# Attention and Fourier block on one core: first keys and queries loaded by themselves, part of it from ScalarE's queue, statistics split

## What is computed

```
xn  = layernorm(x)
q   = rope(xn @ wq)      16 heads of 16 channels
k,v = rope(xn @ wk), xn @ wv     4 heads of 16 channels, query head h uses key head h % 4
a   = softmax(causal(q k^T / 4)) @ v ;  attention = a @ wo
f   = real(ifft(fft(xn) @ (w_re + i w_im))) + bias
out = x + attention + f
```

## Time and profile before

| | us |
|---|---|
| median of three executions | 992.09 |
| the profiled execution | 994.67 |
| its span, first to last instruction | 993.0 |
| TensorE busy in the span | 946.6 |
| VectorE, ScalarE, GpSimd busy | 731.2, 653.1, 312.9 |
| mean granted clock of TensorE | 0.969 |

### The profile page before, as it was taken

One profiled execution on the slowest core, in us unless ns is written; L12 is line 12 of the kernel. 1 busy time (PEld: TensorE's weight loads), 2 busy tenths in 40 slices (PEclk: granted clock), 3 DMA queues, 4 the chain that ended last, 5 costly groups with the idle time before them and its releaser, 6 DMA issues.

```text
span 993.0 us, 17699 instructions
## 1 busy us (share of the span) xinstructions
PE 946.6 (95%) x6764; PEld 463.8 (47%) x6764; DVE 731.2 (74%) x894; ACT 653.1 (66%) x1302; POOL 312.9 (32%) x343
## 2 busy tenths in 40 slices
PE   8969999999999989999999999999999999999998
PEld 6744555445444334534454555444444443544424
DVE  6887677678777897787888666677778887788801
ACT  6423666646667746676777666676677765677795
POOL 4368863865238000136300223236111000100000
PEclk9858999999999989999999999999999997999999
DMA  7535132154101300010100321001410000000000
GB/s 249 134 75 92 34 85 77 34 102 112 50 7 54 60 17 1 13 49 22 49 19 3 69 58 33 22 1 34 104 37 1 2 2 1 13 11 2 1 1 22
DMA packets 37700, 43.48 MB, mean 44 GB/s; under 512 B 11376, under 2 KB 23280, under 8 KB 37616
## 3 DMA queue, kind: packets, MB, share of 16 engines
q1 hardware_dynamic: 37544, 42.35, 17.5%
q10 hardware_dynamic: 72, 0.01, 0.0%
HBM read 27.13 MB, written 14.68 MB: 42 GB/s over the span
## 4 chain that ended last, share of the span: by engine, by line
PE 46%; ACT 4%; issue 1%; DVE 1%; POOL 0%; ACTq 0%; POOLq 0%
PE psO L1387 17%; PE psS L1370 10%; PE psA L1323 10%; ACT prob_sb L986 3%; PE psS L1355 2%; PE psS L1357 1%; PE psA L1328 1%; PE psA L1370 1%; PE psA L1338 1%; PE psS L1296 1%; ACT oraw_sb L995 1%; PE psS L1347 0%; DVE pmax L1132 0%; PE psS L1303 0%; PE psA L1402 0%
## 5 line engine op out<-in xcount | busy, mean ns | idle before, releaser
L986 ACT ACTIVATE prob_sb<-psS 128x512 f32<-128x512 f32 (+2 forms) x1108 | 561.3, 589 | 210.6 <-PE psS L1370 207.7
L1134 DVE TENSOR_REDUCE pmax<-psA 128x2 f32<-128x1024 f32 x384 | 459.9, 1220 | 111.5 <-PE psA L1323 110.4
L1370 PE MATMUL psS<-q_st,k_st 50*128 50x512 f32 (+3 forms) x1232 | 392.1, 425 | 4.6 <-ACT prob_sb L986 3.8
L1323 PE MATMUL psA<-k_st,q_st 48*128 48x512 f32 (+3 forms) x1280 | 360.4, 426 | 16.5 <-DVE pmax L1132 5.6
L1387 PE MATMUL psO<-prob_sb,v_sb 128*17 128x512 f32 (+3 forms) x2560 | 301.7, 543 | 16.2 <-ACT prob_sb L986 7.8
L1323 PEld LDWEIGHTS psA<-k_st,q_st 48*128 48x128 f32 x1280 | 177.5, 193 | 242.0 <-DVE pmax L1134 87.6
L1132 DVE TENSOR_REDUCE pmax<-psA 128x4 f32<-128x512 f32 (+2 forms) x192 | 198.9, 1048 | 88.2 <-PE psA L1328 86.9
L871 POOL TENSOR_SCALAR_AFFINE_SELECT prob_sb<-prob_sb 128x512 f32<-128x512 f32 x128 | 81.1, 636 | 498.6 <-ACT prob_sb L986 484.0
L1370 PEld LDWEIGHTS psS<-q_st,k_st 50*128 50x128 f32 x1232 | 191.2, 188 | 94.1 <-ACT prob_sb L986 83.9
L1387 PEld LDWEIGHTS psO<-prob_sb,v_sb 128*17 128x17 f32 x2560 | 42.9, 95 | 105.1 <-issue 40.2
L1328 PE MATMUL psA<-mask_r,mask_l 64*128 64x64 bf16 (+1 forms) x768 | 81.9, 214 | 0.0
(11 more groups left out here) (110 smaller groups left out, 546.2 us busy)
## 6 DMA issues: line engine op xcount, KB each, us to landing
q_st<-parts_scratch SPq DMA_DIRECT2D x174, 64.0 KB, 2.2
parts_scratch<-parts SPq DMA_DIRECT2D x64, 128.0 KB
k_st<-parts_scratch SPq DMA_DIRECT2D x48, 128.0 KB, 4.3
q_st<-spartT SPq DMA_DIRECT2D x252, 2.0 KB
x_sb<-in_L_attn_x SPq DMA_DIRECT2D x7, 512.0 KB, 4.0
out<-x_sb SPq DMA_DIRECT2D x14, 256.0 KB, 2.2
parts_scratch<-parts SPq DMA_DIRECT2D x32, 64.0 KB
oraw_sb<-in_L_attn_x SPq DMA_DIRECT2D x1, 1536.0 KB, 8.9
```

The lines of the kernel that those rows point to most:

```text
L986: nc.scalar.activation(prob[:, g % DEEP, r0:r0 + hp, s0:CH], bank_at(bank)[:, 0:hp * w].rearrange("p (h s) -> p h s", h=hp), ACT.Exp).then ...
L1134: nc.vector.reduce_max(pmax[:, heads[0]:heads[0] + 3:2, i, q], psA[:, two:two + 2, :], AX.X).then_inc(S["a_free"], 1)
L1323: last = mm(bank[:, k * w:(k + 1) * w], q_st[lo:lo + ROWS, n % (2 * KV), heads[o * per + k] % 2, i * P:(i + 1) * P], k_st[lo:lo + ROWS, sl ...
L1370: last = mm(bank[:, h * w:(h + 1) * w], k_st[lo:lo + FULL, key_slot(n, tile), kv, tile % CT * P:(tile % CT + 1) * P], q_st[lo:lo + FULL, n ...
```

## The change

Five things are changed.

1. **Loads of step 0.** The keys of step 0 are loaded by themselves (`load_first_k(slice(0, 1))`), ahead of the store of part 2; the keys of steps 1 to 3 follow behind store(3). The store of part 2 is split: two of its four DMAs are issued by SP, two by ScalarE, and ScalarE also issues the three loads of the queries of the second half (`first_q(act, 1, False)`), for which it waits until the store of part 2 has landed. ScalarE's `ones_rows(1, ...)`, which stood at these places, go to the end of its opening.
2. **Batch 1's input** (`x_two`, `x_last`) is loaded behind all of these instead of ahead of them.
3. **Statistics.** Tiles 8 to 15 (the rest of batch 0) get samples, moments, root and Newton step before the first use of pass one. Tiles 16 to 31 are sampled behind the shift of step 1, with their moments; their root stands ahead of the first exponent of step 3, and a Newton step follows.
4. **v(0)** leaves the opening and becomes the first side job of the planner. During the uses of step 0 the planner no longer puts a side job in between (`next_a >= LAST_FIRST`).
5. **The planner's figures** are new: SP free at 11 instead of 1, queries of steps 1 to 3 at 8 instead of 7, input of batch 0 at 0 instead of 18, GpSimd free at -5 instead of -6, 6.5 us for the statistics on VectorE. ScalarE has an exponent of one column behind qk(5), before any other exponent.

```diff
-    OPENING += [("rope", 0, 2), ("rope", 1, 2), ("rope", 0, 3), ("rope", 1, 3), ("qk", 3), ("qk", 4), ("qk", 5), ("v", 0)]
+    OPENING += [("rope", 0, 2), ("rope", 1, 2), ("rope", 0, 3), ("rope", 1, 3), ("qk", 3), ("qk", 4), ("qk", 5)]
...
-        pool_free, sp_free, dma_free = -6.0, 1.0, 1.0
+        pool_free, sp_free, dma_free = -5.0, 11.0, 12.0
...
-        q_ready, xnT_at, x_at = {n: 7.0 if n else 0.0 for n in range(KV)}, {0: 0.0, 1: 0.0}, {c: 18.0 for c in range(NJ)}
+        q_ready, xnT_at, x_at = {n: 8.0 if n else 0.0 for n in range(KV)}, {0: 0.0, 1: 0.0}, {c: 0.0 for c in range(NJ)}
...
-        stage = [("v", 1)]
+        stage = [("v", 0), ("v", 1)]
...
             if use == LAST_OF[n]:
                 dve += 0.95
                 issue_dma(dve, ("shift", n))
+                if n == STATS_AT:
+                    dve += 6.5
+                    stats_at.append(dve + 0.1)
...
-                if ready[choice] > first + 1.0 and (beside < BESIDE[step] or ready[choice] == big):
+                if next_a >= LAST_FIRST and ready[choice] > first + 1.0 and (beside < BESIDE[step] or ready[choice] == big):
...
-    ROOTS_JOB = next(job for job in PE_ORDER if job[0] == "b")
+    FIRST_BANK = next(job for job in PE_ORDER if job[0] == "b")
+
+    ROOTS_JOB = ("b", BEGIN[STATS_AT + 2], 0)
...
+        def store_rows(engine, m, half):
+            cc = m // 3
+            w = KV if m % 3 == 0 else 2 * KV
+            at = D if m % 3 == 0 else (m % 3 - 1) * P
+            for part in range(2):
+                rows = scratch[cc, part, at:at + w * HD, :].rearrange("(h m n) s -> m h n s", m=2, n=N8)
+                engine.dma_start(rows[half], parts[half * HALF:half * HALF + w * N8, m % 2, part, :].bitcast(fp32)).then_inc(stored[m % 2], 16)
+
+
+        def first_q(engine, t, rest):
+            m = 1 + t
+            engine.wait_ge(stored[m % 2], 16 * (stores_before(m) + 4))
+            steps = slice(1, KV) if rest else slice(0, 1)
+            at = slice(t * P + 2 * HD, (t + 1) * P) if rest else slice(t * P, t * P + 2 * HD)
+            for row, part in enumerate(PART_ROWS):
+                engine.dma_start(q_st[t * HALF + row * HD:t * HALF + (row + 1) * HD, steps, :, :].rearrange("d g r s -> d (g r) s").bitcast(fp32),
+                                 scratch[0, part, at, :].rearrange("(h d) s -> d h s", d=HD)).then_inc(q_in[1 if rest else 0], 16)
...
+            def store_half(m, half):
+                sp.wait_ge(S["first_parts"], 2 * FIRST.index(m) + 2)
+                store_rows(sp, m, half)
+
+
+            def load_first_k(steps):
+                if steps.start == 0:
+                    sp.wait_ge(stored[0], 16 * (stores_before(0) + 4))
+                    sp.wait_ge(S["ones_first"], 2)
+                for t in range(2):
+                    for row, part in enumerate(KEY_ROWS):
+                        sp.dma_start(k_st[t * HALF + row * HD:t * HALF + (row + 1) * HD, 0, steps, :].bitcast(fp32),
+                                     scratch[0, part, D:D + KD, :].rearrange("(g d) s -> d g s", g=KV)[:, steps, :]).then_inc(k_in[0], 16)
...
+            store(0)
+            store(1)
+            load_first_k(slice(0, 1))
+            store_half(2, 0)
+            first_q(sp, 0, False)
+            store(3)
+            load_first_k(slice(1, KV))
+            first_q(sp, 0, True)
+            first_q(sp, 1, True)
             sp.dma_start(x_two, x_v[:, BTILES:BTILES + TWO, :]).then_inc(S["x_two_in"], 16)
             sp.dma_start(x_last, x_v[:, BTILES + TWO:2 * BTILES, :]).then_inc(S["x_two_in"], 16)
-            store(0)
-            store(1)
-            load_k(0)
-            store(2)
-            load_first_q(0, False)
-            load_first_q(1, False)
-            store(3)
-            for rest in (True,):
-                for t in range(2):
-                    load_first_q(t, rest)
             for job in DMA_ORDER:
...
-                ones_rows(1, m)
+                if m == 0:
+
+                    act.wait_ge(S["first_parts"], 2 * FIRST.index(2) + 2)
+                    store_rows(act, 2, 1)
+                else:
+                    first_q(act, 1, False)
...
+            roots(2 * CT, 4 * CT, 2)
             copy_qk(5)
-            copy_v(0)
+            nc.scalar.activation(aside_sb[:, :], ident[:, 0:1], ACT.Exp)
+            ones_rows(1, 0)
+            ones_rows(1, 1)
             for job in ACT_ORDER:
                 if job == ROOTS_JOB:
+                    roots(4 * CT, CHUNKS * CT, 3)
+                if job == FIRST_BANK:
 
                     act.wait_ge(S["spartT_ready"], 1)
                     rows = q_st[HALF + ROWS:HALF + FULL, 0, :, :].bitcast(fp32).rearrange("o r (i k s) -> o (r i) k s", i=CT, k=CT)
                     for k in range(CT):
                         act.dma_start(rows[:, :, k, :], spartT[32 * k + 16:32 * (k + 1), 0, :]).then_inc(S["shift_in_0"], 16)
-                    roots(2 * CT, CHUNKS * CT, 2)
                 if job[0] == "b":
...
-            sample(2 * CT, CHUNKS * CT)
+            sample(2 * CT, 4 * CT)
+            moments(2 * CT, 4 * CT)
+            newton(2 * CT, 4 * CT, 2)
             for v in range(len(SEQ_A)):
-                if v == LAST_USE[0] + 3:
-                    moments(2 * CT, CHUNKS * CT)
+                if v == LAST_USE[STATS_AT] + 1:
+                    sample(4 * CT, CHUNKS * CT)
+                    moments(4 * CT, CHUNKS * CT)
                 if v == ROOTS_BACK:
-                    newton(2 * CT, CHUNKS * CT, 2)
+                    newton(4 * CT, CHUNKS * CT, 3)
...
-                    if g == 0:
+                    if cc == 0 and g < 2:
+                        pe.wait_ge(k_in[0], 96 * (g + 1))
+                    elif g == 0:
                         pe.wait_ge(k_in[cc], 96)
...
-            project_v(0)
```

More of the change, by code:

```diff
@@ L44, in attention_fourier_block @@
     WARM = (10, 20)
+    STATS_AT = 1
     EPS = 1e-5
@@ L135, in schedule @@
         normed = {}
-        on_at = {}
+        on_at, stats_at = {}, []
         late, ahead = None, 0
@@ L310, in stage_ready @@
                 at = xn_at.get(cc, big)
+                if cc == XS - 1:
+                    at = max(at, stats_at[0] if stats_at else big)
                 if cc >= XS:
@@ L583, in attention_fourier_block @@
         tmp2 = sb("tmp2", [P, CHUNKS * CT], fp32)
+        aside_sb = sb("aside_sb", [P, 1], fp32)
         pmax = sb("pmax", [P, R, CT, NJ], fp32)
@@ L670, in store @@
                     sp.wait_ge(S["parts_done"], 2 * turned_by_pool(m) + 2)
-                cc = m // 3
-                w = KV if m % 3 == 0 else 2 * KV
-                at = D if m % 3 == 0 else (m % 3 - 1) * P
                 for half in range(2):
-                    for part in range(2):
-                        rows = scratch[cc, part, at:at + w * HD, :].rearrange("(h m n) s -> m h n s", m=2, n=N8)
-                        sp.dma_start(rows[half], parts[half * HALF:half * HALF + w * N8, m % 2, part, :].bitcast(fp32)).then_inc(stored[m % 2], 16)
+                    store_rows(sp, m, half)
+            def store_half(m, half):
+                sp.wait_ge(S["first_parts"], 2 * FIRST.index(m) + 2)
+                store_rows(sp, m, half)
+            def load_first_k(steps):
[6 more added lines that the diff above has]
+                                     scratch[0, part, D:D + KD, :].rearrange("(g d) s -> d g s", g=KV)[:, steps, :]).then_inc(k_in[0], 16)
             def load_k(cc):
@@ L701, in load_q @@
                                  scratch[cc, part, at, :].rearrange("(h d) s -> d h s", d=HD)).then_inc(q_in[n % (2 * KV)], 16)
-            def load_first_q(t, rest):
-                m = 1 + t
-                sp.wait_ge(stored[m % 2], 16 * (stores_before(m) + 4))
-                steps = slice(1, KV) if rest else slice(0, 1)
-                at = slice(t * P + 2 * HD, (t + 1) * P) if rest else slice(t * P, t * P + 2 * HD)
-                for row, part in enumerate(PART_ROWS):
-                    sp.dma_start(q_st[t * HALF + row * HD:t * HALF + (row + 1) * HD, steps, :, :].rearrange("d g r s -> d (g r) s").bitcast(fp32),
-                                 scratch[0, part, at, :].rearrange("(h d) s -> d h s", d=HD)).then_inc(q_in[1 if rest else 0], 16)
             def load_shift(n):
@@ L811, in normalise @@
                 pool.wait_ge(x_in[cc % NJ], 16 * (cc // NJ + (CT if cc % NJ == 0 else 1)))
-                pool.wait_ge(S["newton"], 15)
+                pool.wait_ge(S["newton"], 15 if cc < NJ else 20)
                 pool.wait_ge(S["bank_full"], BANK["t", cc - 1, 1] + 1)
```

## The result

Four executions of the changed kernel took 1012.16, 1012.98, 1013.90 and 1017.02 us, a median of 1013.44; the kernel before had 992.97 beside them. The ratio is 1.0175, with an interval of 1.0123 to 1.0226: slower than before, though four executions don't tell whether by more or less than 2%. The forecast was 994, its range 984 to 1001. The profiled execution is that of 1013.90, with a span of 1012.1 us against 993.0.

A forecast was written before the change was run, and what follows sets the result against it. TensorE, busy 95% of the span, was taken as the bound, with the first b's start deciding. Late first b +2.9, work done earlier -1.7, square root +1.3 gave +2.5 us on the median of 992.09: 994.6, rounded to 994, range 984 to 1001.

The forecast's parts named there:

- First maxima at 41.6: Opening: the store of part 2 lands 3.2 us earlier, so TensorE's first maxima start at 41.6 against 44.13.
- Queries of steps 1 to 3 at 53: Opening: these queries land at about 53, so step 1 begins 3.2 us earlier than before.
- the same lag gives 52.9: Opening: queries of steps 1 to 3 land 7.4 us behind their last issue at about 45.5, as before.
- v, t and the shift: Before the first b: two v take 3.8 to 7.3 us, ScalarE's shift leaves late, first b at 69.8, 2.9 later.
- Square root, +1.3: ScalarE near 110 us: two more table loads of 1.28 us, half counted, +1.3, bounds 0 and 2.6.
- Statistics, "cost 0, upper bound 3 if reductions of step 2 are then missed": VectorE from 62 to 68.5: moved samples and moments fit the hole before the first b, cost 0, at most 3.
- The half-clock stretch, "counted at 0, bounds -3 and +3": Opening: TensorE's stretch at 1.2 GHz shifts with the first b, counted at 0, bounds -3 and +3 us.
- Rival C: After the first b: half clock lasts beyond 95 us, costing 5 us on 994.6, so 1000; chance 0.13.
- "Other orders of TensorE later on (...) can add or take some 3 us": Behind the opening: the planner's new orders can add or take some 3 us, judged from one place near 365 us.

The follow-up runs named there:

- e16: Kernel before with the new loads, x_two and x_last first, and queries and keys of step 1 loaded ahead of steps 2 and 3; 1001.18 us, ratio 0.9989.
- e1: Changed kernel with ScalarE's four shift transfers of step 0 moved ahead of its copies of t(2,0) and t(2,1); 1016.06 us, ratio 1.0129.
- e4: Changed kernel with the last 16 roots taken as a plain copy, so no table is loaded in the middle; 1013.55 us, ratio 1.0100.
- e17: Changed kernel with other planner figures and the side-job rule of before, an order with 1384 a-b neighbours against 1362; 1002.57 us, ratio 1.0065.
- e18: Changed kernel with other planner figures, an order with 1337 a-b neighbours against 1362; 1028.00 us, ratio 1.0267.
- e14: Changed kernel measured again, unchanged, beside the kernel before on another chip; 1016.89 us, ratio 1.0183.
- e9: Changed kernel with the loads of the kernel before, order and split statistics as changed; 1018.67 us, ratio 1.0173.
- e7: Changed kernel with filler matmuls in four stretches ahead of clock falls, ahead of b(0,0), and at two later falls; 1007.85 us, ratio 1.0081.
- e6: Changed kernel with three filler matmuls of 512 columns ahead of the first score matmul b(0,0); 1015.02 us, ratio 1.0143.

## Why the prediction was wrong

- **First maxima at 41.6** (bounds 40.5 and 44.1): 43.36. The store of part 2 landed at 38.0, as forecast, and the three issues on ScalarE took 1.3 us for the 1.9 counted. The landing was mis-sized: from the end of the last issue to TensorE's first use it was 43.36 - 39.36 = 4.0 us, not the 1.9 of before. SP was issuing store(3) and the other keys beside them; that this is the reason isn't tested.
- **Queries of steps 1 to 3 at 53, "the same lag gives 52.9"**: 56.76. From the last issue (44.82) it was 11.9 us, not 7.4; e16, which puts the bytes of step 1 first, has it at 50.5. The counts of their semaphore show why: the six transfers land one after another, some 1.5 us apart, in before (49.15 to 56.15) as in the changed kernel (48.05 to 56.71), so the place in the line decided and not the issue.
- **v, t and the shift**: the two v took 7.09 us at half clock, both t came before the first b, ScalarE's transfers left at 67.08, the first b came at 71.27 for 69.8. Right in mechanism; but in e1, which takes this wait away, nothing comes back that can be told.
- **Square root, +1.3** (0 to 2.6): e4 shows nothing of it, and can't tell 1.3 us from 0.
- **Statistics, "cost 0, upper bound 3 if reductions of step 2 are then missed"**: this term failed. By themselves they are 1.0108, some 10 us, of which 2.6 lie above the line; the rest is clock. In the changed order samples and moments are hidden by the hole ahead of the first b (VectorE 64.84 to 71.5, TensorE idle to 71.27), as was argued; whoever fills that hole meets them. The Newton step, which the sum doesn't price at its new place, isn't hidden: 3.12 us of idle TensorE, and a fall of the clock behind it.
- **The half-clock stretch, "counted at 0, bounds -3 and +3"**: for the opening that held, 41.0 us against 37.5. It failed behind it: falls at 108.5, 125.6 and 169.9 us, 27 us long together, the second behind that idle time, the third with TensorE busy all through. Rival C had the right kind of cause at the wrong place: its sign, the clock still at 0.5 at 95, did not come.
- **"Other orders of TensorE later on (...) can add or take some 3 us"**: this is the step that decided. It stood outside the sum, and was read from one place near 365 us. From job a(183,0) on, which runs at about 350 us before and 370 in the changed kernel, both have the same order; up to there the changed one has 20 neighbours fewer (365 against 385) and the three new falls, and is 20 us late. Orders of the same work span 1002.6 to 1028 us (e17, e18). The term should have been a range of +-12. Counting neighbours would have hinted at its sign.

The parts do not add: statistics 1.0108, loads 1.0016, statistics and loads in the old order 1.0102, with the changed order 1.0100 to 1.0183 (changed, e14, e1, e4, e9). What is shown is that the statistics cost by themselves, that the loads don't, and that the order moves the changed kernel by more than the intervals (e17 at 1.0065, e18 at 1.0267). How many of the 19 us belong to the order and how many to the statistics is open, and so is whether an order costs by its clock or by what runs side by side. The order without the split statistics wasn't tried, since both t ahead of the first b need the first part of them.

## What to carry to other kernels

Where a planner decides anew from changed figures, the new order is a change of its own: compare the two orders, and give it a term from the scatter of other orders before you price the opening. Move work off an engine's free stretch only to where that engine is free again; 5.4 us of samples that cost nothing ahead of the first maxima held TensorE idle for 6.6 between two of them, and its clock down for 20 us more. Follow every piece of the moved work to its new place, the small last one too. Filler matmuls took half clock away here, but no kernel with them was shown to beat the one before: they are work themselves (17.5 us in e7). And before you believe the releaser that a row names, look when its transfers landed: a semaphore that two loads share points at the wrong one.

## What the runs showed of the hardware

The granted clock of the changed kernel fell from 2.4 to 1.2 GHz at 169.9 us without a gap ahead of it: from 166 to 170 TensorE was busy for 3.97 of 4.00 us, with score matmuls of 48 and 50 rows and the small mask matmuls alone. It stayed down until 183.6 with TensorE full (170 to 180: 10.00 of 10), score and PV matmuls in about equal parts. The fall at 125.6 came behind 3.12 us of idle TensorE. The Trainium skill (TensorE: Matmul & The Clock Gate, "Why this matters for your kernels") names idle gaps between bursts as what takes the clock down; the fall at 125.6 agrees, the one at 169.9 goes further. And 7.09 us of back-to-back matmuls of 128 rows by 64 columns (the two v) did not lift it, while it rose in e6 behind two t and 0.8 us of matmuls of 512 columns. The same program differs by up to 34 us between executions (991.55 to 1025.93), which follow the line given above: the time at 1.2 GHz accounts for it within some 1.2 us.
